# Attention block of an early-fusion transformer layer on one core: a weighted sum moved between two remainders, and the work orders of the quantized products and of the experts' inputs changed

## The reference, cut to what matters

```
h = concat(patch_embedding(x), text_embedding(x_txt))      # 32 examples, 25 + 128 tokens, 192 channels
h = h + attention(layernorm(h))      # 12 heads of 16, 8-bit activations and weights
h = h + ffn(layernorm(h))            # 3 experts of 768, top 1 per example, exact gelu

# attention
xq  = fq_act(x); wq = fq_weight(w); qkv = fq_act(xq @ wq.T + b)
a   = fq_act(q @ k.T * 16**-0.5)
r   = x_int - x0_int * floor(x_int / x0_int)          # the remainder of an integer exponential
e   = floor((r * (r + b_int) + c_int) * 2**(30 - q))  # a square of r, times a power of two
w   = 2**-round_log2(sum(e) / e)                      # 4-bit logarithmic softmax
out = fq_act(w @ v); out = fq_act(out @ fq_weight(proj_w).T + proj_b)

# ffn
scores = softmax(mean(x, tokens) @ Wg.T); sel = top_1(scores)
y = (gelu(x @ W1[sel] + b1[sel]) @ W2[sel] + b2[sel]) * scores[sel]
```

## Time and profile before

| | |
|---|---|
| median of 3 runs | 1025.52 us (1023.57 to 1028.31) |
| the profiled execution, its own time | 1024.34 us |
| its span, first to last instruction | 1022.5 us |
| busy in the span | PE 704.2, DVE 870.8, ACT 709.0, POOL 171.0 us |
| granted TensorE clock, mean | 0.849 |
| `quant_qkv` in the trace | about 166 to 227 us |
| `attention` | about 350 to 758 us |
| `ffn_inputs` | about 798 to 852 us |

### The profile page before, as it was taken

One profiled execution on the slowest core, in us unless ns is written; L12 is line 12 of the kernel. 1 busy time (PEld: TensorE's weight loads), 2 busy tenths in 40 slices (PEclk: granted clock), 3 DMA queues, 4 the chain that ended last, 5 costly groups with the idle time before them and its releaser, 6 DMA issues. The chain is left out here.

```text
span 1022.5 us, 23611 instructions
## 1 busy us (share of the span) xinstructions
PE 704.2 (69%) x6531; PEld 475.1 (46%) x6532; DVE 870.8 (85%) x2388; ACT 709.0 (69%) x1376; POOL 171.0 (17%) x276
## 2 busy tenths in 40 slices
PE   3783387747888467766677756677635384999997
PEld 3562144434655333333344333343323254999896
DVE  6888997888888889999999999999978854677766
ACT  0345365966888799999898999999944393554553
POOL 5851320006665100000000000000005530000000
PEclk9986598988999787789777797777857697999999
DMA  8000000001111111111111111111021004455452
GB/s 259 3 2 0 0 1 1 0 0 37 37 37 37 40 28 25 24 25 28 24 25 24 25 26 24 24 24 24 13 105 64 18 1 155 144 192 199 163 193 90
DMA packets 84272, 54.72 MB, mean 54 GB/s; under 512 B 53704, under 2 KB 83176, under 8 KB 83976
## 3 DMA queue, kind: packets, MB, share of 16 engines
q1 hardware_dynamic: 83208, 54.11, 17.4%
q0 software_dynamic: 1024, 0.13, 0.2%
HBM read 11.90 MB, written 3.76 MB: 15 GB/s over the span
## 5 line engine op out<-in xcount | busy, mean ns | idle before, releaser
L1365 DVE SCALAR_TENSOR_TENSOR expo<-expo,con,pow 128x153 f32<-128x153 f32 x480 | 146.2, 376 | 0.7 <-ACT expo L1275 0.7
L1149 PE MATMUL at_rem<-word,ident_half 128*128 128x459 f16 x160 | 68.7, 430 | 104.6 <-ACT expo L1275 102.5
L1275 ACT ACTIVATE expo<-at_rem,con 128x459 f32<-128x459 f32 x160 | 98.8, 645 | 17.3 <-PE at_rem L1150 13.0
L952 DVE TENSOR_REDUCE rs_ends<-rs_banks 128x770 f32 (+1 forms) x96 | 89.2, 958 | 12.7 <-PE rs_banks L924 10.3
L1401 DVE CUSTOM_DVE_ANT_0 weight_top<-weight_top,line 128x2448 uint16<-128x2448 uint16 x64 | 85.6, 1352 | 6.4 <-ACT line L1267 4.5
L873 ACT ACTIVATE rs_banks<-rs_banks 128x770 f32<-128x770 f32 x96 | 74.3, 796 | 22.9 <-PE rs_banks L916 21.8
L1149 PEld LDWEIGHTS at_rem<-word,ident_half 128*128 128x128 f16 x160 | 15.7, 98 | 152.7 <-ACT expo L1275 146.7
L1238 ACT ACTIVATE word<-at_banks 128x459 uint8<-128x459 f32 x160 | 79.6, 560 | 8.5 <-PE at_banks L779 5.5
L1231 ACT ACTIVATE pT_all<-at_pT 128x768 bf16<-128x768 int16 (+3 forms) x160 | 78.9, 562 | 8.3 <-PE at_pT L1173 2.5
L1907 ACT ACTIVATE qk<-e_p,b1s 128x153 f32<-128x153 f32 x192 | 58.7, 393 | 28.4 <-PE e_p L1868 27.3
L1868 PE MATMUL e_p<-X,qk 128*128 (+1 forms) x960 | 71.8, 234 | 7.3 <-DMA qk<-vt 6.9
(11 more groups left out here) (387 smaller groups left out, 2040.7 us busy)
## 6 DMA issues: line engine op xcount, KB each, us to landing
qk<-vt SPq DMA_DIRECT2D x64, 384.0 KB, 3.1
rs_kb<-qk SPq DMA_DIRECT2D x128, 28.7 KB, 1.9
kb<-qk SPq DMA_DIRECT2D x128, 28.7 KB, 1.9
patches<-in_patches SPq DMA_DIRECT2D x4, 768.0 KB
vi<-vt SPq DMA_DIRECT2D x32, 96.0 KB, 2.0
out<-vi SPq DMA_DIRECT2D x32, 96.0 KB, 1.9
pj_w<-in_w SPq DMA_DIRECT2D x1, 2304.0 KB, 8.5
qb<-qk SPq DMA_DIRECT2D x128, 6.0 KB, 1.8
```

Source lines behind the costliest of these rows:

```text
L952: v.tensor_reduce(ends[:, :, n, 5 * b:5 * b + 5], banks[:, slot(u, b), :, 0:5 * W].rearrange("p i (t n) -> p i t n", n=W), AX, ALU.max).th ...
L1149: pe.matmul(out, identh[:, :], bank(word, b).bitcast(F16), start=True, stop=False)
L1275: act.activation(bank(ex, b), rem[:, (u + b) % 2, 0:3 * N], ACT.Square, scale=2.0 ** 24, bias=c(5)).then_inc(sq_done, 1)
L1365: ins = v.scalar_tensor_tensor(ex[:, t, :], ex[:, t, :], c(7), pw[:, t, :].bitcast(BF16), ALU.add, ALU.mult, accum_out=tot[:, t:t + 1])
```

## The change

In `quant_qkv` the hardware loop over chunks is written out on PE and DVE. The second chunk's q products follow the first's before the wait for the rows; DVE limits the first chunk's q before it copies the rows. The four image products stand after chunks 2, 5, 8 and 11, on PE behind the q product of the next chunk. ACT's loop is as before.

In `attention` PE makes remainders 0 and 1, then the weighted sum, then remainders 2 to 4.

In `ffn_inputs` the last group's token sums stand before the low parts of the last but one and before the last turn. DVE normalizes three tiles of the last group instead of one, ACT two instead of four, and DVE copies out one of the four high parts of the last but one group. An exponential of a constant stands at the start of ACT's list, and the gate's exponential comes after the last but one group's low parts instead of ahead of the last group's.

```diff
 # quant_qkv
+        AFTER = tuple(3 * g + 2 for g in range(G // 2))
+        image_of = lambda i: AFTER.index(i) if i in AFTER else None
+        turn_of = lambda i: i + sum(1 for x in AFTER if x < i)
 # PE
-                def body(i, z):
-                    pe.wait_ge(vrows, 2)
-                    pe.wait_ge(v_scaled, i + 1)
-                    v_product(z, lambda w, kt: xqT[:, kt, ds(i * W + w * N, NT)])
-                    if not (isinstance(i, int) and i == NCH - 1):
+                def text_values(i):
+                    n = turn_of(i)
+                    pe.wait_ge(v_scaled, n + 1)
+                    v_product(n % 2, lambda w, kt: xqT[:, kt, i * W + w * N:i * W + w * N + NT])
+
+                def image_values(i, g):
+                    n = turn_of(i) + 1
+                    pe.wait_ge(v_scaled, n + 1)
+                    v_product(n % 2, lambda w, kt: xqI[:, kt, (2 * g + w) * P:(2 * g + w + 1) * P])
+
+                q_product(1)
+                pe.wait_ge(vrows, 2)
+                for i in range(NCH):
+                    text_values(i)
+                    if 0 < i < NCH - 1:
                         q_product(i + 1)
-                chunks(pe, body)
-                for g in range(G // 2):
-                    pe.wait_ge(v_scaled, NCH + g + 1)
-                    v_product(g % 2, lambda w, kt: xqI[:, kt, (2 * g + w) * P:(2 * g + w + 1) * P])
+                    if image_of(i) is not None:
+                        image_values(i, image_of(i))
 # DVE
+                for u in range(2):
+                    q_limit(0, u)
                 v.wait_ge(row_ps, 1)
...
+                for i in range(NCH):
+                    n = turn_of(i)
+                    if i > 0:
+                        q_limit(i, 0)
+                    v_scale(n % 2, n)
+                    if i > 0:
+                        q_limit(i, 1)
+                    v_shift(n % 2, n)
+                    v_limit(n % 2, n, vt[...], V_UNIT, True)
+                    if image_of(i) is not None:
+                        g, n = image_of(i), n + 1
+                        v_scale(n % 2, n)
+                        v_shift(n % 2, n)
+                        v_limit(n % 2, n, vi[...], unit[:, 0:1], False)
 # attention, PE
                     if now is not None:
-                        remainder(n, u, range(NB))
+                        remainder(n, u, range(2))
                     if last is not None:
                         weighted(*last)
+                    if now is not None:
+                        remainder(n, u, range(2, NB))
 # ffn_inputs
+        shared = lambda g: g == G - 2
+        ahead = lambda g: 3 if g == G - 1 else 1
 # PE
                 def token_sums(g):
+                    pe.wait_ge(xn_ok, G + g + 1)
+                    pe.wait_ge(xn2_ok, g + 1)
                 def low_parts(g):
                     pe.wait_ge(hi_ok, g + 1)
+                    if shared(g):
+                        pe.wait_ge(xn2_ok, 2 + g + 1)
...
                 for g in range(G):
+                    if g + 2 == G:
+                        token_sums(g + 1)
+                        low_parts(g)
+                        turn(g + 1)
+                        continue
 # ACT
-                    for w in range(1, 5):
+                    for w in range(ahead(g), 5):
...
-                        act.activation(out[:, :, 0:NT], text, ACT.Copy)
+                        if not (part == 0 and kt == 1 and shared(g)):
+                            act.activation(out[:, :, 0:NT], text, ACT.Copy)
...
+                act.wait_ge(made, 2)
+                act.activation(warm[:, :], ones[:, 0:1], ACT.Exp).then_inc(eready, 1)
...
-                    if g == G - 1:
+                    parts(g, 1, (lo_ps, g + 1), lo_ok)
+                    if g == G - 2:
                         exponential()
-                    parts(g, 1, (lo_ps, g + 1), lo_ok)
 # DVE
+                    for w in range(ahead(g)):
+                        ins = v.tensor_scalar(xn[:, g % 2, w, :], Hres[:, 4 * g + w, :], ...)
+                def high_parts(g):
+                    v.wait_ge(xt_ps, G + g + 1)
+                    v.tensor_copy(tokens(0, 1, g)[:, :, 0:NT], turned(g, 1)[0]).then_inc(xn2_ok, 1)
...
                 offsets(G - 1)
+                high_parts(G - 2)
```

More of the change, by code:

```diff
@@ L642, in q_product @@
                                 mm = pe.matmul(pq[:, u, t, 0:W], wqT[:, kt, (3 * u + t) * P:(3 * u + t + 1) * P],
-                                               xqT[:, kt, ds(i * W, W)], start=(kt == 0), stop=(kt == 1))
+                                               xqT[:, kt, i * W:(i + 1) * W], start=(kt == 0), stop=(kt == 1))
                         mm.then_inc(q_prod, 1)
@@ L702, in _, with q_limit @@
                     v.memset(unit[32 * j:32 * j + ID, :], 0.0).then_inc(unit_set, 1)
+                def q_limit(i, u):
+                    v.wait_ge(q_int, i * 2 + u + 3)
+                    v.tensor_scalar(qk[:, i * 2:i * 2 + 2, 3 * u:3 * u + 3, :].rearrange("p b t n -> p t b n"),
+                                    qi[:, u, :, :].rearrange("p t (b n) -> p t b n", n=N), cap, None, ALU.min).then_inc(q_done, 1)
+                for u in range(2):
+                    q_limit(0, u)
                 v.wait_ge(row_ps, 1)
@@ L708, in _ @@
                 both = lambda j: rows[:, j, :].unsqueeze(1).to_broadcast([P, 2, C])
[L710 to L713, removed]
                 def v_scale(z, n):
@@ L726, in v_limit @@
                     v.tensor_scalar(out, whole, cap, scale, ALU.min, ALU.mult).then_inc(v_done, 1)
[L728 to L734, removed]
-                v.wait_ge(unit_set, 4)
[L736 to L739, removed]
+                v.wait_ge(unit_set, 4)
+                for i in range(NCH):
[6 more added lines that the diff above has]
+                    v_shift(n % 2, n)
+                    v_limit(n % 2, n, vt[:, i * 2:i * 2 + 2, :].rearrange("p w (r x f) -> p (w r) x f", x=4, f=HD)[:, :, 0:4:3, :], V_UNIT, True)
+                    if image_of(i) is not None:
+                        g, n = image_of(i), n + 1
+                        v_scale(n % 2, n)
+                        v_shift(n % 2, n)
+                        v_limit(n % 2, n, vi[:, 2 * g:2 * g + 2, :].rearrange("p w (h f) -> p (w h) f", f=32)[:, :, 0:HD], unit[:, 0:1], False)
 class Stage:
@@ L1587, in ffn_inputs @@
         minus, ones, each, wg, products = sb("f_minus", [P, P], BF16), sb("f_ones", [32, P]), sb("f_each", [P, 2 * B - 1 + 2 * B - 4]), sb("f_wg", [32, E, C]), sb("f_products", [32, C])
+        warm = sb("f_warm", [32, 1])
         lg, mx, tot, inv, hit, pick, spread = (sb("f_" + x, s) for x, s in (("lg", [32, E]), ("mx", [32, 1]), ("tot", [32, 1]), ("inv", [32, 1]),
@@ L1698, in exponential @@
                 def exponential():
-                    act.wait_ge(eready, 1)
+                    act.wait_ge(eready, 2)
                     act.activation(lg[:, :], lg[:, :], ACT.Exp, accum_out=tot[:, :]).then_inc(edone, 1)
+                act.wait_ge(made, 2)
+                act.activation(warm[:, :], ones[:, 0:1], ACT.Exp).then_inc(eready, 1)
                 normalize(0)
@@ L1743, in offsets @@
                         v.wait_ge(summed, g - 1)
-                    v.tensor_scalar(xn[:, g % 2, 0, :], Hres[:, 4 * g, :], mv[:, g, 0, 0:1], rstd[:, g, 0:1], ALU.subtract, ALU.mult).then_inc(xn2_ok, 1)
+                    for w in range(ahead(g)):
+                        ins = v.tensor_scalar(xn[:, g % 2, w, :], Hres[:, 4 * g + w, :], mv[:, g, w, 0:1], rstd[:, g, w:w + 1], ALU.subtract, ALU.mult)
+                    ins.then_inc(xn2_ok, 1)
+                def high_parts(g):
+                    v.wait_ge(xt_ps, G + g + 1)
+                    v.tensor_copy(tokens(0, 1, g)[:, :, 0:NT], turned(g, 1)[0]).then_inc(xn2_ok, 1)
                 for g in range(G):
```

## The result

Timed against each other, the changed kernel takes 1021.22 us and the kernel before 1023.57 (medians of eleven runs). The means, without one stray execution of 1611.08 us, are 1020.62 and 1024.52; the ratio is theirs: 0.9962, interval 0.9943 to 0.998, so 3.9 us or 0.38 per cent less. That is within the 0.5 per cent that I called no change, and outside my range of 1009.5 to 1020.5. The profiled execution of the changed kernel took 1023.18 us, 2 us over its median, with a span of 1021.4.

A forecast was written before the change was run, and what follows sets the result against it. No single engine was taken to bound the whole: ACT paces `quant_qkv`, DVE bounds `attention`, ACT and the gate chain meet in `ffn_inputs`. Terms -3.9 - 3.0 - 2.8 = -9.7 us from 1024.34 gave 1014.6, forecast 1015.0, range 1009.5 to 1020.5.

The forecast's parts named there:

- the start: Start of `quant_qkv`: chunk 1's products follow at 172.05 and ACT at 173.05, 1.5 us earlier.
- the first wait: Start of `quant_qkv`: ACT waits 0.5 us for DVE's limit of chunk 1 before it can fill that part again.
- the wait behind an image: `quant_qkv`: each image triple on DVE makes ACT wait 0.75 us, 3.0 for four.
- Rival D: `quant_qkv`: DVE becomes the bound and each image costs ACT 1.47 us; 0 to -1 there, 1018 in all; chance 0.07.
- Rival E: `ffn_inputs`, at the gate: the table load returns or low parts hold ACT up; -1.5 there, 1016 in all; chance 0.07.
- One bound of mine: `quant_qkv`: with no wait at the images, 7 us less 0.5 of the start, a gain of 6.4.
- the third term: `attention`: moving the weighted sum gives fewer falls of the clock, 40 per cent of an excess of 7.3 us: -3 us.
- my own marks: `attention` profile signs: steps' mean 12.15 us, clock's mean above 0.8, L1401's waits for the line fewer than 13.
- Behind remainder 4 PE stands ready sooner: `attention`: the scores that follow wait for ACT's first byte anyway, so PE being ready sooner is worth nothing.
- C: `attention`: the sum delays remainder 2, the third square, ACT and DVE's line; steps of 12.6, about 1029 us; chance 0.05.
- A: `attention`: the clock gives nothing, since the 2.3 us gap before the sum lets it fall; -6.7, 1018 us; chance 0.20.
- B: `attention`: the clock stays up nearly always and all steps take 12.02 us; -14, 1010.5 us; chance 0.12.

The follow-up runs named there:

- the later sum: The changed kernel with attention's weighted sum one place later, between the third and fourth remainder; 0.9997 of the kernel before.
- both gaps filled: The changed kernel with five unread matmuls ahead of the weighted sum and five behind remainder 4; 1011.48 us, 0.9872 of the kernel before.
- the kernel before with its fill: The kernel before, old order, with five unread 128-wide matmuls between remainders 1 and 2; 1016.99 us, 0.9947 of the kernel before.

## Why the prediction was wrong

**What held.** In `quant_qkv` the start (1.5 us forecast, 1.62 less idle time), the first wait (0.5; it was 0.32), the wait behind an image (0.75; 0.73) and DVE's end behind ACT (1.6; 1.55) are each where I put them, and the stage gives 3.7 us for 3.9. Rival D falls with that. In `ffn_inputs` I forecast 2.8 and the stage's own length gives 2.8. The stage now begins 799.30 - 797.98 = 1.32 us later in the trace; less that, the last sums end at 841.86 (forecast 841.8), the exponential starts at 844.16 (844.15), DVE takes its result at 844.48 (844.5) and the stage ends at 849.49 (849.5). That it fits to a tenth is in part luck, as the spread of this stage between profiles shows. Rival E falls. The Trainium skill, "ScalarE: Activation LUTs" (What ACT_TABLE_LOAD costs), counts 1283 ns for the load and another 1380 for a drain, 2.66 us for every switch. The trace agrees with the load, 1.28 us in the earlier trace rows, and shows no drain: the exponential starts at 846.94, where the load ends, and the copy ahead of the load ends at 845.63. The stage's gain of 2.8, with the spread named above, is also nearer to what I had worked out with 1.28 than to the 1.4 us more of the page's figure. One bound of mine was off: with no wait at the images `quant_qkv` would have given 3.9 + 3.0 = 6.9 us, not 6.4, since the start's 0.5 was already in the 3.9.

**The step that failed** is the third term, "I expect fewer falls of the clock", and with it "I take 40 per cent: -3 us". Measured, the order costs 1.5 to 2.5 us instead of giving 3. Put that in the sum: -3.9 - 2.8 + 2 = -4.7, against 3.9 less measured. Of my own marks the mean clock (0.80), the mean step (12.42 from total to total, for 12.15) and the waits of DVE for the line (18 for 13) all came out on the other side. Three things were wrong in it.

First, I priced the clock by its falls. They did become fewer, 27 to 24, and the mean clock stayed, 0.81 and 0.80, and yet the steps grew. In the old order the falls come some 4 to 7 us behind the reciprocal, many half-clock stretches are over before 10.6 us, and 206 of 1248 turning matmuls run slow. In the new order they come at 4.5 to 8.2 us, all last into the turn, and it is 606. In the turn PE is dense and ACT stands right behind it. The step at 0.72 took 12.01, but it was not free: its half clock reached over the turn, and the step behind it took 12.53. A stretch that ends ahead of the turn can be free. In the old order with its gap filled and both stages new, one lies from 521.6 to 525.0, and the step in which it lies and the next both take 12.01:

```profile
516.10:528.11 12.01, 8.81 (x88) 4.53 (x88) 11.96 (x41) 10.72 (x21) 0.00 (x0) 0.86 0.11 25
528.11:540.12 12.01, 8.22 (x93) 4.49 (x92) 11.96 (x41) 11.49 (x24) 0.00 (x0) 1.00 0.12 26
```

```profile
522.67 1.41 ACT L1293 ACTIVATE expo<-at_rem,con 128x459 f32<-128x459 f32 x2 [0.51 <-PE at_rem L1160]
...
532.00 2.61 DVE L1419 CUSTOM_DVE_ANT_0 weight_top<-weight_top,line 128x2448 uint16<-128x2448 uint16 x2
```

That the turn is the channel rests on the ranks' wait (2.5 to 8.3 us in the change, 8.5 with the later sum, 1.0 with both gaps filled) and on the single kernels above. With the gap behind remainder 4 filled only 101 turning matmuls run slow, and the step still takes 12.16; there ACT's bytes wait 5.7 us for their scores, against 2.1 in the kernel before with its fill, and most of that is the fill itself at half clock, as shown. What the longer wait for scores costs in the change, 8.7 us for 5.5, I did not take apart from the turn.

Second, "Behind remainder 4 PE stands ready sooner …: nothing". The sum left a hole there: 1.19 us of idle PE before the scores (0.55 with the sum in place), while the first gap shrank only from 2.94 to 2.37. I wrote that "a new gap of some 1.2 us opens behind remainder 4", with the right size, and gave it no price. Filling that hole alone takes the clock from 0.80 to 0.90 and the time from 0.9962 to 0.992. Moving PE's work from one gap to another does not fill a gap, it trades them.

Third, the reading that the term started from. I wrote that at half clock ACT waits 0.51 us for a remainder ("and again for scores"), "so it comes late to the line, and DVE waits 0.26 us for it". The rows just shown have the same wait of 0.51 for a remainder, and DVE's sum with the line in the next step waits for nothing: the wait for the remainder is not what makes the line late. In the rows of the changed kernel the late line stands behind late turns, and in the kernel filled behind remainder 4 the long step stands behind late scores.

**The rivals.** C had the right sign and a mark that was passed, a mean over 12.4 from total to total (12.42). But its mechanism, the squares waiting for remainder 2, isn't what happened: that wait fell from 13.0 to 11.2 us, and the order is free at full clock. A, with nothing from the clock, was with D the nearest in time, at 1018, and still too low, since it too allowed the order no loss. The time itself lies in the case that I gave 0.03, several small losses (1020 to 1023); it was one loss in one term. B's price was right: steps of 12.02 are to be had, and with both gaps filled they were, 12.02 to 12.04, but not by moving the sum. The Trainium skill, "TensorE: Matmul & The Clock Gate" (HAM oscillation), blames the idle gap between bursts and asks for short ones. The trace agrees once the gap is filled (clock 0.90 and 0.96). A gap that is 0.6 us shorter and has a second beside it left it at 0.80, so the longest gap is not the thing to look at by itself.

**The sum.** I forecast 9.7 us less for the change, and it gave 3.9. Of the 5.8 between, 4.5 to 5.5 are the order (3 that didn't come, 1.5 to 2.5 that it cost). The rest is within the intervals.

## What to carry to other kernels

A move of TensorE work is to be priced by the clock that the *dense, awaited* stretch will have, not by the number of falls or the mean: ask which stretch has another engine right behind it, and how far ahead of it the idle time ends. Work moved out of a gap leaves one, and it has to go into the sum too. Before an order is tuned for the clock it is worth filling the gaps with unread matmuls as a test, all of them at once: one gap filled left the question open here, both filled showed that the order was harmless and the clock was not. The filled kernels were also the faster ones. A fill has its own price where it runs at half clock ahead of work that is awaited.

## What I had not expected of the hardware

Unread matmuls pay: five in a gap, 1.24 us of PE's time where it idles, take the clock of the stage from 0.81 to 0.90 and 5.4 us from the kernel, 0.53 per cent. Their width does not matter, 32 columns of weights or 128 (0.9943 and 0.9947, clock 0.90 in both). And the same half clock may cost nothing or 0.7 us, by its place, and the bill may come a step later: a step at a mean of 0.86 and the one behind it both took 12.01 us, while a step at 0.97 took 12.74 because half clock lay over the turn ahead of it.
